# Scan stage: the vector engine makes the whole product of u and B, GpSimd makes half of the product of h and C

## The reference, cut to what matters

```python
half_dA = 0.5 * delta[..., None] * A
denom_inv = 1.0 / jnp.maximum(1.0 - half_dA, STAB_EPS)
A_bar = (1.0 + half_dA) * denom_inv
B_bar = jnp.sqrt(delta)[..., None] * Bp[:, :, None, :] * denom_inv
Bx = B_bar * xn[..., None]

def step(h, inp):
    a_t, bx_t, c_t = inp
    h = a_t * h + bx_t
    y_t = jnp.einsum('bdn,bn->bd', h, c_t)
    return (h, y_t)
...
y = jnp.moveaxis(ys, 0, 1) + D_skip * xn
```

## Time and profile before

| what | value |
|---|---|
| median of 3 runs | 5811.28 us (5802.47 to 5816.74) |
| the profiled execution, its own time | 5814.46 us |
| its span in the trace | 5813.0 us |
| the four scan stages in it | about 1066 us together |
| mean granted clock of PE | 0.961 of full |

### The profile page before, as it was taken

How to read it: one execution, slowest core, us unless ns; L and a number is a source line. 1 busy time by engine, 2 the same in 40 slices (tenths; PEclk the granted TensorE clock), 3 DMA queues, 4 the chain that set the end, 5 groups by cost and what they waited for, 6 DMA issues and landing times. The chain is left out here.

```text
span 5813.0 us, 94556 instructions
## 1 busy us (share of the span) xinstructions
PE 5028.4 (87%) x32123; PEld 2145.5 (37%) x32123; DVE 4317.1 (74%) x5419; ACT 3426.4 (59%) x5923; POOL 1419.5 (24%) x885
## 2 busy tenths in 40 slices
PE   5777777777767999996999999999999999999995
PEld 3233233233234566652333333333333333333334
DVE  5997987987971111115888888888888888888884
ACT  5765765666631111112767777777777777777772
POOL 1855846846850000004750000000000000000005
PEclk8998998998998999997999999999999999999998
DMA  3303003002022211213331111111111111111114
GB/s 100 106 15 116 0 28 104 1 30 87 1 78 83 72 61 62 65 61 86 101 87 32 34 30 29 29 29 34 32 29 29 29 32 34 29 29 29 29 39 163
DMA packets 351454, 299.33 MB, mean 51 GB/s; under 512 B 169184, under 2 KB 320992, under 8 KB 350432
## 3 DMA queue, kind: packets, MB, share of 16 engines
q1 hardware_dynamic: 336192, 251.90, 15.2%
q0 software_dynamic: 14848, 42.09, 2.4%
HBM read 175.78 MB, written 117.57 MB: 50 GB/s over the span
## 5 line engine op out<-in xcount | busy, mean ns | idle before, releaser
L1448 ACT ACTIVATE at_E<-at_ps 128x512 f32<-128x512 f32 x4096 | 2146.4, 604 | 836.3 <-PE at_ps L1356 821.3
L1465 DVE TENSOR_REDUCE at_mpart<-at_ps 128x1 f32<-128x1024 f32 x2080 | 2445.0, 1217 | 250.4 <-PE at_ps L1343 233.4
L1356 PE MATMUL at_ps<-at_qs,at_ks 98*128 98x512 bf16 x4096 | 1243.4, 385 | 19.7 <-ACT at_E L1448 17.1
L1364 PE MATMUL at_ps<-at_E,at_vst 128*32 128x256 f32 x16400 | 1101.7, 386 | 0.0
L1341 PE MATMUL at_ps<-at_ks,at_qs 64*128 64x512 bf16 x2080 | 697.1, 389 | 172.8 <-DVE at_A L1490 79.4
L1343 PE MATMUL at_ps<-at_kb,at_qb 64*128 64x512 bf16 x2080 | 697.2, 389 | 0.0
L1565 POOL TENSOR_TENSOR at_f<-at_f,at_sig 128x1024 f32<-128x1024 f32 x16 | 37.1, 2348 | 2696.3 <-ACT at_sig L1595 2696.3
L854 POOL TENSOR_TENSOR l_work<-l_work 128x1024 f32<-128x1024 f32 x256 | 604.5, 2361 | 78.7 <-DVE l_work L863 69.6
L1356 PEld LDWEIGHTS at_ps<-at_qs,at_ks 98*128 98x128 bf16 x4096 | 315.4, 97 | 832.3 <-ACT at_E L1448 572.4
L1364 PEld LDWEIGHTS at_ps<-at_E,at_vst 128*32 128x32 f32 x16400 | 428.7, 109 | 410.7 <-ACT at_E L1448 184.6
L750 PE MATMUL l_ps<-l_bc,l_sel 96*128 96x512 bf16 x1024 | 313.3, 395 | 289.3 <-DVE l_work L863 126.8
(11 more groups left out here) (199 smaller groups left out, 4573.9 us busy)
## 6 DMA issues: line engine op xcount, KB each, us to landing
at_ks<-kp SPq DMA_DIRECT2D x396, 64.0 KB
ff_xin<-xd SPq DMA_DIRECT2D x41, 512.0 KB, 4.4
xd<-l_zero SPq DMA_DIRECT2D x4, 5120.0 KB, 33.2
yd<-ff_yout SPq DMA_DIRECT2D x40, 512.0 KB, 3.2
at_qs<-qp SPq DMA_DIRECT2D x132, 128.0 KB
at_qb<-qp SPq DMA_DIRECT2D x132, 128.0 KB
ff_w<-in_eW SPq DMA_DIRECT2D x9, 1024.0 KB, 5.8
at_kb<-kp SPq DMA_DIRECT2D x264, 32.0 KB
```

The lines of the kernel that those rows point to most:

```text
L1356: pe.matmul(S[chunk_bank(u, l)], m.ks[0:STACK + 2, j, bass.ts(kt, P)], m.qs[0:STACK + 2, j, half * QB + hf * BANK:half * QB + (hf + 1) * B ...
L1364: mm = pe.matmul(O[32 * q:32 * q + 32, :], m.vst[:, par, 2 * sl + kk, :], m.E[:, sl % 4, kk, bass.ts(q, QG)], start=(sl == 0 and kk == 0), ...
L1448: act.activation(m.E[:, sl % 4, c // 2, bass.ts(c % 2, BANK)], S[chunk_bank(u, l)], ACT.Exp, scale=SCALE).then_inc(s.ex, 1)
L1465: dve.tensor_reduce(m.mpart[:, job:job + 1], ring[n % 2].rearrange("p a b -> p (a b)"), AX_X, ALU.max).then_inc(s.ring_free, 1)
```

## The change

DVE's `weigh` makes all 1024 columns of `w`, from both banks of `pB`. DVE's product `hc` makes only the first 512 columns, and POOL makes the other 512 behind the scan, from `h` and from a copy of half of C in SBUF. ACT no longer copies half of B (`b_out`), but half of C (`c_out`). The semaphores `wa`, `wb` become one, `w`; `hc` becomes two, `hca` (DVE's half) and `hcb` (POOL's half); `b_sbuf` becomes `c_sbuf`. The order on ACT and POOL changes with it.

```diff
                 def spread_c(i):
                     if i:
-                        pe.wait_ge(s.hc, i)
+                        pe.wait_ge(s.hca, i)
+                        pe.wait_ge(s.c_sbuf, i)
                     spread(pC, n + NS, t0).then_inc(s.c_psum, 1)
...
-                    pe.wait_ge(s.hc, i + 1)
-                    for q in range(2):
+                    for q, made in ((0, s.hca), (1, s.hcb)):
+                        pe.wait_ge(made, i + 1)
                         mm = pe.matmul(y[:, q, :], m.ident[:], hc[i % 2][:, bass.ts(q, BANK)],
...
-                def b_out(i):
-                    act.wait_ge(s.b_psum, i + 1)
+                def c_out(i):
+                    act.wait_ge(s.c_psum, i + 1)
                     if i >= 2:
-                        act.wait_ge(s.wb, i - 1)
-                    act.copy(Bs[i % 2], pB[:, 1, :]).then_inc(s.b_sbuf, 1)
+                        act.wait_ge(s.hcb, i - 1)
+                    act.copy(Cs[i % 2], pC[:, 1, :]).then_inc(s.c_sbuf, 1)
...
                 for i in range(2):
-                    b_out(i)
                     inverse(i)
                 for i in range(UNITS + 1):
                     if i < UNITS:
                         decay(i)
+                        c_out(i)
                     if i:
                         carry(i - 1)
                     if i + 2 < UNITS:
-                        b_out(i + 2)
                         inverse(i + 2)
                     if i >= NS and i % NS == 1:
                         y_out(i - 2)
...
+                def product(i):
+                    pool.wait_ge(s.w, i + 1)
                     pool.wait_ge(s.inv, i + 1)
                     if i >= 2:
                         pool.wait_ge(s.h, i - 1)
                     pool.tensor_tensor(bx[i % 2], w[i % 2], inv[i % 2], ALU.mult).then_inc(s.bx, 1)
+                def result(i):
+                    pool.wait_ge(s.h, i + 1)
+                    pool.wait_ge(s.c_sbuf, i + 1)
+                    if i >= 2:
+                        pool.wait_ge(s.y_added, i - 1)
+                    pool.tensor_tensor(hc[i % 2][:, HI], h[i % 2][:, HI], Cs[i % 2], ALU.mult).then_inc(s.hcb, 1)
+                product(0)
+                product(1)
+                for i in range(UNITS):
+                    result(i)
+                    if i + 2 < UNITS:
+                        product(i + 2)
...
-                    dve.tensor_tensor(w[i % 2][:, LO], m.u[:, k, t0:t0 + BANK], pB[:, 0, :], ALU.mult).then_inc(s.wa, 1)
+                    dve.tensor_tensor(w[i % 2], m.u[:, k, t0:t0 + HALF], flat(pB), ALU.mult).then_inc(s.w, 1)
...
                     if i >= 2:
-                        dve.wait_ge(s.hc, i - 1)
+                        dve.wait_ge(s.hcb, i - 1)
+                        dve.wait_ge(s.hca, i - 1)
...
-                    dve.tensor_tensor(hc[i % 2], h[i % 2], flat(pC), ALU.mult).then_inc(s.hc, 1)
+                    dve.tensor_tensor(hc[i % 2][:, LO], h[i % 2][:, LO], pC[:, 0, :], ALU.mult).then_inc(s.hca, 1)
```

More of the change, by code:

```diff
@@ L715, in scan_batch @@
     with ExitStack() as ctx:
-        s = stage_sems(nc, ctx, f"scan{b}", "x_in zeroed b_psum c_psum b_sbuf inv decay wa wb bx h hc y_added carried y_out")
+        s = stage_sems(nc, ctx, f"scan{b}", "x_in zeroed b_psum c_psum c_sbuf inv decay w bx h hca hcb y_added carried y_out")
         work = lambda n: m.work[:, bass.ts(n, HALF)]
         inv, w, bx, h, hc = ([work(2 * n), work(2 * n + 1)] for n in range(5))
-        Bs = [m.work[:, 10 * HALF:10 * HALF + BANK], m.work[:, 10 * HALF + BANK:11 * HALF]]
+        Cs = [m.work[:, 10 * HALF:10 * HALF + BANK], m.work[:, 10 * HALF + BANK:11 * HALF]]
         flat = lambda pair: pair[:].rearrange("p a b -> p (a b)")
@@ L756, in spread_b @@
                     if i:
-                        pe.wait_ge(s.wa, i)
-                        pe.wait_ge(s.b_sbuf, i)
+                        pe.wait_ge(s.w, i)
                     spread(pB, n, t0).then_inc(s.b_psum, 1)
```

## The result

The changed kernel takes 5829.9 us in the median of 7 runs (5827.8 to 5841.9), against 5811.3 for the kernel before (5800.8 to 5818.3). The ratio is 1.0038 with a 95% interval of 1.0026 to 1.0050: slower by 22 us in the mean (15 to 29) and by 18.6 us between the medians. Forecast were 5842.5 us, 5825 to 5864. The profiled execution of the changed kernel took 5841.9 us, the slowest of its seven.

What follows compares the result with a forecast made beforehand. DVE was taken to bound ordinary units, and a chain through ACT and PE the boundaries. Ordinary units 0, boundaries +20.2, clock +13.2, starts 0, ends -2.2 sum to +31.2 us on 5811.3: 5842.5 us, range 5825 to 5864.

Steps and rivals of the forecast that it cites:

- What bounds it: Scan stages: DVE is full and never waits in ordinary units, 3.91 or 3.97 us each; boundaries follow a chain.
- ordinary units: Units between boundaries: spacing stays 3.91 and 3.97 us, 0 us change, with 0.2 us of room on POOL and ACT.
- Boundaries later and longer: Twelve boundaries: `y_out` behind `c_out` delays `skip` and the next scans, 1.92 or 1.56 us each, +20.2 us.
- The clock: TensorE before `skip`: the gap grows from 1.5 to 2.8 us, clock falls at all twelve boundaries, +13.2 us.
- Start and end: Of each batch: first scans 0.6 to 0.8 us sooner but net 0; the end saves 0.54, -2.2 us in all.
- The late boundaries without the clock: Rival at the boundaries: all terms but the clock's, +18.0 us, 5829 us; within the 0.3% bound, chance 0.13.
- what the forecast claimed for itself: Whole kernel: the forecast case, slower, 5829 to 5856 us, chance 0.71.
- Ordinary units didn't stretch: Rival in ordinary units: POOL's or ACT's round becomes longer; 0.1 us per unit adds 25.6 us, 5868 us, chance 0.11.
- Nor did the clock fall in them: Rival in ordinary units: TensorE's clock falls there too and PE binds, +330 us, 6140 us, chance 0.02.

Runs made afterwards that it cites:

- e8: The changed kernel with half of C copied twice on ACT in every unit, first to unused space; 5873.2 us, 1.0110 to the kernel before.
- e3: The changed kernel with four extra matmuls adding zeros into y before `skip` at each boundary; 5811.3 us, 1.0000 to the kernel before.
- e1: The changed kernel with `y_out` moved ahead of the copy of C on ACT at the boundaries; 5771.2 us, 0.9934 to the kernel before.
- e2: The changed kernel with ACT's copy of C moved behind carry and inverse, `y_out` still last; 5782.7 us, 0.9954 to the kernel before.
- the repeat: The changed kernel run again, unaltered; 5831.5 us, 1.0045 (1.0032 to 1.0059) to the kernel before.
- e5: The kernel before the change, with `y_out` right behind the decay at the boundaries; 5773.2 us, 0.9939 to the kernel before.
- e4: The kernel before the change, with y first copied to unused space just ahead of `y_out`; 5832.5 us, 1.0036 to the kernel before.
- e6: The changed kernel with `y_out` right behind the decay at boundaries and the copy of C last on ACT; 5773.1 us, 0.9942 to the kernel before.

## Why the prediction was right, and where it was off

**What bounds it, and ordinary units: right.** Ordinary units take 3.91 and 3.97 us after the change, as before, and DVE doesn't wait in them. The decay starts at 2.41 and not at 2.50, since inverse starts 0.10 behind the carry (187.67 to 187.77) where I had added 0.18. Those 0.18 were misread: in the earlier trace rows the copy behind the carry starts 0.64 after the spread of B (185.58 to 186.22), which fits a wait for B and not the carry's own length. e8 gives the room.

**Boundaries later and longer: right, and shown.** Worked out were +20.2 us. `skip` at 7.46 and 7.36 was measured at 7.37 and 7.34. e3, with its late falls and its later `skip` taken out, gives 38.0 - 1.4 - 2.2 - 15.0 = 19.4 us for the order (15.0 is what the twelve boundaries of the kernel before cost at full clock, 4 x 1.32 + 8 x 1.22), and the three units at full clock within 0.2 us of the sum; e1 shows that the place of `y_out` is the cause, and e2 that the queue behind the late copy is the rest of it.

**The clock: the mechanism right, the size off, and the step that failed is the one that compared with a single trace.** In the two first traces it is nearly as worked out: the boundaries grew by 34.7 us, 20.2 for the order and 14.5 for the clock, where I had 13.2; all twelve are down. But "5 of 12" was one draw. In three traces of the kernel before, the boundaries cost 24.0, 33.2 and 32.1 us, of which the clock's part is what is above 15.0, on average 14.7, and in the changed one 23.5, or about 24 by e3. The term is +9 and not +13.2. That the first pair of traces agrees so well with the sum (1098.6 - 1065.9 = 32.7 for 31.2) is in part luck: against the other two traces of the kernel before it would be 22.4 and 23.1. With 8.8 the sum is 20.2 + 8.8 - 2.2 = 26.8 us, inside the measured 15 to 29, and inside the 19 to 34 of the repeat (1.0045). The first forecast of 31.2 lies just above the first interval.

**Start and end: right.** The end gains 0.53 us a batch, 2.1 in all (2.2). At the start the first scan begins 2.0 us sooner in the first batch and 0.9 in the others (0.6 to 0.8 were forecast), and by the fourth scan the gain over four batches is 0.2 us in all, as "nothing" had it.

**The rivals.** The late boundaries without the clock (5829) come out at the measured median, but not by their mechanism: the clock fell at all twelve. The measured median also lies at the lower edge of what the forecast claimed for itself, 5829 to 5856. Ordinary units didn't stretch. Nor did the clock fall in them. By the rule on micro-idles (the Trainium skill, TensorE: Matmul & The Clock Gate, on a second failure mode) it would have swung there, and the traces are against it: TensorE has two gaps of 0.46 and 0.53 us in a unit before the change and one of 0.99 to 1.05 after it, and the granted clock stays at 1.00. Where it fell, a gap of 1.5 us or more was close by.

**What stays open.** The timed runs have no trace. That the clock falls at about 8 boundaries in the typical run of the kernel before is inferred from two of three profiles. The medians speak for it: when the stages of each altered kernel and of both traces of the changed one are taken back by the difference of the medians (for e5, 1042.1 + 5808.7 - 5773.2 = 1077.6 us), the nine estimates of the stages of the kernel before lie between 1068 and 1085, 1077 on average, where its three traces had 1065.9, 1076.2 and 1075.5. And the parts outside the scan differ by up to 31 us between traces of kernels that are equal there; their cause wasn't tried.

## What to carry to other kernels

An exchange of equal work between engines leaves the steady loop as it is and is decided at its seams: ask what now stands ahead of the rare instruction (here `y_out`), and put it where its engine waits anyway, which was worth 0.6% here for a move of two lines. Price a late operand by what is queued behind its reader. And before a term rests on how often the clock fell in one trace, take a second trace.

## What the runs showed of the hardware that was not expected

The granted clock of TensorE fell although its longest single gap was 1.5 us (1.6 in e2): with a `skip` 6.15 to 6.3 us after the scan it fell at 5, 8, 8 and 7 of 12 boundaries, in otherwise equal units. With a `skip` at 7.06 or later, and a gap of 2.4 us or more ahead of it, it fell at all of 12 in each of four traces (the changed kernel twice, e4, e8); with gaps of 1.1 us and below ahead of `skip`, at none of 12 in four traces (e1, e3, e5, e6). The length of a single gap doesn't settle it, though: a gap of 2.0 us some 9 us behind `skip` was followed by a fall at 8 of 12 boundaries in e3, but only at 1 and 2 of 12 in the two traces of the changed kernel. Nor does a fall always cost: in the changed kernel the clock also fell in unit 4 of every batch, after a gap of 2.0 us, and no scan there was late by more than 0.12 us. The falls ahead of or just behind `skip`, where the chain runs through TensorE, cost 1.8 to 2.3 us each on average over a trace. And adding four matmuls, 1.9 us of work, at each boundary made the kernel 0.3% faster than it was without them (5811.3 for 5829.9), since they kept the clock at 2.4 GHz for the work right behind them.
